# A written-out order of steps whose planner charges for a change between parts of TensorE's array

## The chip, the cores and the metric

The kernel runs on one core of one Trainium2 chip. The metric is the device time in microseconds (us) of one execution; lower is better. PE is the matmul engine (TensorE), DVE is VectorE, ACT is ScalarE, POOL is GpSimd, SP issues DMAs.

## What is computed

The input is x of shape (16, 256, 128), float32. Six parts follow each other, each added to x (LN is a layer norm without weights):

```
x = x + 0.5 * FFN(LN(x))        # ternary weights 128 -> 512 gated (silu * linear), 512 -> 512 gelu, 512 -> 512 gelu, 512 -> 128
x = x + ATT0(LN(x))             # linear attention, no softmax: (theta x)(phi x)^T g(x) / sqrt(128)
x = x + 0.5 * FFN(LN(x))        # the same weights again
x = x + 0.5 * MOE(LN(x))        # 8 low-rank experts, top 2, gates from the first token of each batch
x = x + ATT1(LN(x))             # 16 heads of width 8, rotary, causal softmax over 256 tokens
x = x + 0.5 * MOE(LN(x))
```

## The kernel before

The 16 batches are cut into 8 chunks of 512 tokens (two batches each). The feed-forward layers run as two interleaved streams of chunks; each fp32 product is two matmuls of a rounded high part and a rest (lines 921 and 925). The softmax attention works per batch u in steps of two heads.

Nothing in the kernel decides at run time what comes next. A planner, class `Order`, lays one list of 1,848 steps on the host, and every engine walks this list in the same order and issues its own part of each step, with semaphore waits where data or a buffer is needed. So the list fixes the order on each of the five queues. The planner holds a clock for each engine (`P` for PE, `V` DVE, `A` ACT, `G` POOL, `S` SP). Jobs stand in a list by fixed priorities (a smaller number first; feed-forward about 3, the first pass over the scores 5.5 or 6.5, the maxima 5.2, the second pass 6, the end of a batch 6.6). `run` takes the first job that can go on at the time of `clock["P"]`, the job calls `put` for a step, and `put` moves the clocks by the durations in `TAKES` (for each engine: how long it is held, and how long until the result is there). Whether a bank of PSUM is free, whether a source is done and whether DVE's or ACT's queue is short enough (`pair`: the engine's clock less than `QUEUED` = 1.0 us ahead) are all asked against `clock["P"]`. The kind of array part that a step uses is not asked by any job.

The steps that the change speaks of:

- `pass1` (lines 1075, 1079, 1082), 128 times: 8 bf16 matmuls of 64 or 48 rows for two heads; they use half of the array's rows. DVE then takes the row maxima (line 1315, about 0.95 us) and so empties two banks.
- `pass2` (line 1110), 128 times: 4 bf16 matmuls of 50 rows, the scores transposed, with the maxima as extra rows. ACT takes the exponential (line 1450), POOL masks it (line 1533).
- `weigh` (line 1123), 64 times: 8 fp32 products, 16 matmuls as the trace counts them, of 128 rows and 32 columns: a quarter of the array's columns. They multiply the probabilities with the values for four heads.
- everything else on PE uses the whole array (for instance `upright`, line 1132; `flat`, line 1139; `proj`, 1145; `qk`, 1060; `xta` and the like, 940; `expert`, 1053). `max_out` (line 1099) has 32 columns, but the planner counts it with the whole array.
- `reloc` (DMAs of line 1589): loads K and Q of a batch from DRAM into one of four buffers, ahead of its `pass1` steps; `TAKES` gives it 2.95 us of SP and 5.0 us of DMA.
- `keep` (line 1093): filler. `fill` looks at the stretch in which the planner has PE idle before a step, and lays `int((gap - 0.15) * 0.65 / 0.06)` matmuls of 128x128 on the whole array into it when that is over 1. They compute nothing that is used. `fill` inserts them without passing through `put`, so they move no clock and don't alter `self.pe`, the kind of the last step.

The banks: six banks of PSUM serve as three pairs for the two passes, two more serve all small steps.

Of the kernel before, what the change touches and what calls it, by code (L numbers as in the profile page):

```python
# [30 lines left out]
class Step:  # L31
# [57 lines left out]
COMES = {"stat": [3.5], "cast_v": [5.6, 12.6], "cast_a": [7.1, 8.5, 10.6]}  # L89

BESIDE = ("norm",)
KINDS = {"up": "r", "hid": "r", "down": "r", "pass1": "h", "pass2": "h"}
TABLES = {"silu": "silu", "gelu": "gelu", "pass2": "exp"}
AHEAD = 0.0
KEPT = 4
# [25 lines left out]
class Order:  # L121
# [36 lines left out]
    def put(self, name, **k):  # L158
        n = self.count.get(name, 0)
        self.count[name] = n + 1  # L160
        if name in ("up", "hid", "down"):
            self.into[k["s"]] += 1
            self.lasts = k["s"]
        elif name == "xtf":
            self.into[k["s"]] = 0
        st = Step(name, n, **k)
        self.steps.append(st)
        src = list(st.src) if isinstance(st.src, (list, tuple)) else [st.src]
        if name in ("hid", "down"):
            src = src[st.x:st.x + 2]  # L170
        ready = max([s.at["A"] if s.name in ("cast0", "cast1") else s.done for s in src if s is not None]
                    + [self.left(st.emptied)])
        later = self.left(st.emptied2)
        if n < len(COMES.get(name, ())):
            ready = max(ready, COMES[name][n])
        t = ready
        late = name + "_late" if self.dead and name + "_late" in TAKES else name
        if name == "up" and not self.opened:
            late = "up_first"
        for i, (eng, us, *way) in enumerate(TAKES[late]):  # L180
            if eng == "D":
                t += us
                continue
            if eng == "P":
                kind = KINDS.get(name, "f")
                self.clock["P"] += 0.08 * (kind != "h" and self.pe == "h")
                self.pe = kind
            if eng == "A":
                table = "gelu" if name == "tanh" and self.table == "silu" else TABLES.get(name, self.table)
                self.clock["A"] += 1.29 * (table != self.table)  # L190
                self.table = table
            if i or name == "up":
                t = max(t, later - 0.45 * (name == "up"))
            s0 = max((ready if name in BESIDE else t) + HOPS[eng], self.clock[eng])
            if eng == "P":
                self.fill(s0)
                self.idle_from = s0 + us
            self.note(eng, s0, s0 + us, name)
            self.clock[eng] = s0 + us
            t = st.at[eng] = s0 + way[0]  # L200
        st.done = max([t] + [st.at[e] for e in st.at if name in BESIDE])
        return st
# [1483 lines left out]
```

## Time and profile before

| what | us |
| --- | --- |
| median of 3 runs | 686.41 (686.03 to 687.04) |
| profiled execution, first to last instruction (span) | 684.8 |
| what lies around the span, taken as the median less the span | 1.6 |
| PE busy in the span | 642.0 |
| feed-forward stretch, to the first `pass1` | 0 to 411 |
| attention stretch | 411 to 684.8 |

The profile records no time for its execution other than the span; the 1.6 us of starting and ending are the difference from the median of the runs. Matmuls overlap in the array, so the busy time of PE overstates how long a step holds it. What a step costs is read as the distance from its first start to the next step's first start, in places where PE waited for nothing.

### The profile page before, as it was taken

The page shows a single profiled execution, that of the slowest core. Times are in us where ns is not written, and L with a number is a line of the kernel's source. Part 1 is how long each engine was busy: PE and PEld are TensorE (multiplying, and loading weights), DVE is VectorE, ACT ScalarE, POOL GpSimd, SP SyncE. Part 2 cuts the span into 40 slices and gives each one's busy share as a digit, 9 for nine tenths or more (in the row PEclk, how much of TensorE's full clock was granted, in tenths as well). Part 3 has the DMA queues.
Part 4 walks back from the last instruction along what each step waited for, and adds up shares of the span by engine and source line. Part 5 has one row for each costly group of instructions (what it writes and reads, how often), then busy time and mean ns, then how long its engine had stood idle before and what let it go on. Part 6 is the DMA issues. An engine that isn't in the chain of part 4 may idle for free.

```text
span 684.8 us, 14480 instructions
## 1 busy us (share of the span) xinstructions
PE 642.0 (94%) x5407; PEld 484.4 (71%) x5407; DVE 497.3 (73%) x1300; ACT 493.2 (72%) x846; POOL 300.3 (44%) x461
## 2 busy tenths in 40 slices
PE   4899999999999999999999999889989899999995
PEld 2687878888887878887788877555556565666664
DVE  6767476577566686668786688998897678877455
ACT  5799688778778878877887685248666776567660
POOL 1412121232133363135383637568777653554660
PEclk9999999999999999999999999999999999999999
DMA  9200000000000011000020264414243322112001
GB/s 296 82 1 1 1 0 1 2 0 1 1 0 1 1 46 47 1 1 1 24 69 13 78 199 129 130 48 155 72 151 94 113 93 66 64 49 66 18 2 48
DMA packets 41655, 37.11 MB, mean 54 GB/s; under 512 B 2880, under 2 KB 36960, under 8 KB 41584
## 3 DMA queue, kind: packets, MB, share of 16 engines
q1 hardware_dynamic: 41584, 36.17, 16.9%
q8 instruction: 44, 0.72, 0.4%
q14 instruction: 27, 0.22, 0.1%
HBM read 21.21 MB, written 14.68 MB: 52 GB/s over the span
## 4 chain that ended last, share of the span: by engine, by line
PE 59%; DVE 19%; ACT 10%; issue 6%; DMA 3%; SPq 1%; POOL 1%; DVEq 1%; ACTq 0%; POOLq 0%
PE PSA L921 19%; PE PSA L925 18%; DVE MX L1315 6%; PE PSA L1123 4%; DMA QS<-dq 3%; DVE G L1187 3%; PE PSA L940 3%; PE PSA L1110 2%; ACT PSA L1361 2%; PE PSA L1075 2%; ACT G L1357 2%; PE PSA L1060 1%; ACT PB L1450 1%; DVE RA L1308 1%; PE PSA L1053 1%
## 5 line engine op out<-in xcount | busy, mean ns | idle before, releaser
L1315 DVE TENSOR_REDUCE MX<-PSA 128x6 f32<-128x768 f32 x128 | 118.7, 950 | 25.3 <-PE PSA L1082 24.9
L921 PE MATMUL PSA<-ah,WH 128*128 128x512 f32 x320 | 130.0, 406 | 0.5 <-DVE G L1187 0.5
L925 PE MATMUL PSA<-al,WH 128*128 128x512 f32 x320 | 125.2, 391 | 0.0
L1361 ACT ACTIVATE PSA<-PSA,SC 128x512 f32<-128x512 f32 x128 | 84.7, 662 | 55.0 <-PE PSA L925 54.5
L1450 ACT ACTIVATE PB<-PSA 128x768 f32<-128x768 f32 x128 | 100.7, 815 | 12.8 <-PE PSA L1110 12.5
L921 PE MATMUL PSA<-bh,WH 128*128 128x512 f32 x256 | 104.8, 410 | 2.7 <-DVE G L1187 2.3
L1533 POOL TENSOR_SCALAR_AFFINE_SELECT PB<-PB 128x512 f32<-128x512 f32 x128 | 80.5, 635 | 54.6 <-ACT PB L1450 52.6
L925 PE MATMUL PSA<-bl,WH 128*128 128x512 f32 x256 | 100.3, 392 | 0.0
L1479 POOL TENSOR_SCALAR VE<-MV 128x4 f32<-128x4 f32 x46 | 10.9, 237 | 195.3 <-DVE MV L1162 195.3
L1192 DVE TENSOR_TENSOR al<-PSA,ah 128x512 fp32r<-128x512 f32 x64 | 44.0, 688 | 52.6 <-ACT ah L1368 52.2
L921 PEld LDWEIGHTS PSA<-ah,WH 128*128 128x128 f32 x320 | 60.4, 189 | 13.1 <-issue 0.7
L925 PEld LDWEIGHTS PSA<-al,WH 128*128 128x128 f32 x320 | 60.4, 189 | 12.0 <-issue 0.7
L1192 DVE TENSOR_TENSOR bl<-PSA,bh 128x512 fp32r<-128x512 f32 x64 | 44.0, 688 | 33.6 <-ACT bh L1368 33.3
L1187 DVE SCALAR_TENSOR_TENSOR G<-PSA,SC,G 128x512 f32<-128x512 f32 x64 | 46.8, 748 | 29.6 <-ACT G L1357 22.8
L1489 POOL TENSOR_SCALAR XN<-X,MV,RS 128x128 f32<-128x128 f32 x78 | 62.7, 812 | 3.1
L921 PEld LDWEIGHTS PSA<-bh,WH 128*128 128x128 f32 x256 | 48.1, 188 | 14.0 <-DVE G L1187 4.9
L1123 PE MATMUL PSA<-PB,VA 128*32 128x256 f32 (+1 forms) x1024 | 54.5, 331 | 2.1 <-POOL PB L1533 0.4
L925 PEld LDWEIGHTS PSA<-bl,WH 128*128 128x128 f32 x256 | 48.2, 188 | 8.9 <-issue 0.2
L921 PE MATMUL PSA<-XH,WH 128*128 128x512 f32 x128 | 53.2, 416 | 1.4 <-DVE XL L1182 1.4
L1463 ACT ACTIVATE OT<-PSA 128x256 f32<-128x256 f32 x64 | 24.7, 386 | 38.1 <-PE PSA L1123 38.0
L925 PE MATMUL PSA<-XL,WH 128*128 128x512 f32 x128 | 51.1, 399 | 0.0
L1481 POOL TENSOR_TENSOR RS<-VE,MHALF 128x4 f32<-128x4 f32 x46 | 48.4, 1053 | 3.8
(148 smaller groups left out, 1354.3 us busy)
## 6 DMA issues: line engine op xcount, KB each, us to landing
KS<-dk SPq DMA_DIRECT2D x32, 192.0 KB
QS<-dq SPq DMA_DIRECT2D x32, 192.0 KB
dk<-CB SPq DMA_DIRECT2D x16, 192.0 KB, 2.6
dq<-CB SPq DMA_DIRECT2D x16, 192.0 KB, 2.3
X<-in_x SPq DMA_DIRECT2D x8, 256.0 KB, 6.8
dk<-CB SPq DMA_DIRECT2D x16, 128.0 KB, 2.1
dq<-CB SPq DMA_DIRECT2D x16, 128.0 KB, 1.9
VA<-in_ones SPq DMA_DIRECT2D x4, 512.0 KB
```

Of the source, the lines that this page charges most:

```text
L921: e.matmul(o, WH[:, col:col + 128], hi, start=first, stop=False)
L925: return e.matmul(o, WH[:, col:col + 128], low, start=False, stop=last)
L1123: t = e.matmul(PSA[32 * v:32 * v + 32, b, 128 * k:256], V[:, k, 4 * g + v, :], P[:, 1, :] if k else P[:, 0::2, :], start=(k == 0), stop=(k ...
L1187: e.scalar_tensor_tensor(out=G[:, i, :], in0=bank(b), scalar=SC[:, 4 + st.j:5 + st.j], in1=G[:, i, :], op0=ALU.mult, op1=ALU.mult).then_in ...
L1192: e.tensor_tensor(cut(PL_[st.s, dst], st.j), h, cut(PH_[st.s, dst], st.j), ALU.subtract).then_inc(v_lo, 1)
L1315: e.tensor_reduce(MX[:, u % 2, 1:4, :].rearrange("p t (l g) -> p l t g", l=2)[:, :, :, g], PSA[:, b:b + 2, 0:384].rearrange("p l (t k) -> ...
L1361: e.activation(bank(b), bank(b), ACT.Gelu, scale=SC[:, k:k + 1]).then_inc(a_gelu, 1)
L1450: e.activation(PB[:, n % 4, :, :, :].rearrange("p t l q -> p l t q"), PSA[:, b:b + 2, 0:384].rearrange("p l (t q) -> p l t q", t=3), ACT.E ...
L1463: e.activation(OT[u % 2][:, g, :], PSA[:, b, 0:256], ACT.Copy).then_inc(a_ot, 1)
L1481: e.tensor_tensor(RS[:, i, :], VE[:, i, :], MHALF[:, :], ALU.pow).then_inc(g_rs, 1)
L1489: t = e.tensor_scalar(XN[:, i, j, :], X[:, 4 * c + j, :], MV[:, i, j, 0:1], RS[:, i, j:j + 1], ALU.subtract, ALU.mult)
L1533: e.affine_select(out=P, in_=P, compare_op=ALU.is_ge, fill=0.0, base=0, pattern=[[0, 4], [1, 128]], channel_multiplier=-1).then_inc(g_sel, 1)
```

## The change

Three things change in the planner, none in what a step does:

1. Before, `put` moved PE's clock on by 0.08 us when a step that isn't `pass1` or `pass2` followed one of these. Now it moves it by 0.094 us whenever the kind of the part differs from that of the step before, in either direction, with three kinds: half (`pass1`, `pass2`), quarter (`weigh`), whole (all others).
2. `pass1` is planned 0.01 us shorter on PE (0.34), `pass2` 0.01 us shorter (0.17).
3. `weigh` is planned 0.10 us shorter on PE (0.69), and its result 0.08 us earlier (0.78).

The entries `up`, `hid` and `down` of the old table had the kind "r", which only had to differ from "h".

```diff
--- before.py
+++ after.py
@@ -75,10 +75,10 @@
     "cast1": [("A", 0.52, 0.62), ("S", 0.95, 0.95), ("D", 2.5)],
     "rest1": [("G", 1.12, 1.16), ("S", 0.95, 0.95), ("D", 2.3)], "reloc": [("S", 2.95, 2.95), ("D", 5.0)],
     "value": [("P", 0.83, 1.05), ("A", 0.48, 0.59)], "vexp": [("A", 0.31, 0.41)], "ones": [("S", 1.5, 1.5), ("D", 6.0)],
-    "pass1": [("P", 0.35, 0.51), ("V", 0.868, 0.95)], "peak": [("V", 0.14, 0.22), ("A", 0.13, 0.24), ("G", 0.2, 0.26)],
+    "pass1": [("P", 0.34, 0.51), ("V", 0.868, 0.95)], "peak": [("V", 0.14, 0.22), ("A", 0.13, 0.24), ("G", 0.2, 0.26)],
     "max_out": [("P", 0.22, 0.29), ("V", 0.2, 0.27), ("S", 1.18, 1.18), ("D", 3.8)],
-    "pass2": [("P", 0.18, 0.34), ("A", 0.69, 0.81), ("G", 0.59, 0.63)],
-    "weigh": [("P", 0.79, 0.86), ("A", 0.27, 0.38)], "upright": [("P", 0.45, 0.6), ("V", 0.5, 0.58)],
+    "pass2": [("P", 0.17, 0.34), ("A", 0.69, 0.81), ("G", 0.59, 0.63)],
+    "weigh": [("P", 0.69, 0.78), ("A", 0.27, 0.38)], "upright": [("P", 0.45, 0.6), ("V", 0.5, 0.58)],
     "flat": [("P", 0.27, 0.44), ("A", 0.27, 0.38)], "proj": [("P", 0.64, 0.71), ("V", 0.33, 0.41)], "store": [("S", 0.9, 0.9)],
     "half_stat": [("V", 0.7, 0.8)], "half_power": [("G", 1.1, 1.1)], "half_norm": [("V", 0.45, 0.5)], "half_xt": [("P", 0.2, 0.6), ("A", 0.27, 0.38)],
     "half_logit": [("P", 0.2, 0.4), ("V", 0.5, 0.6)], "half_tanh": [("A", 0.09, 0.2)], "half_pick": [("V", 1.3, 1.4)],
@@ -89,7 +89,7 @@
 COMES = {"stat": [3.5], "cast_v": [5.6, 12.6], "cast_a": [7.1, 8.5, 10.6]}
 
 BESIDE = ("norm",)
-KINDS = {"up": "r", "hid": "r", "down": "r", "pass1": "h", "pass2": "h"}
+TILES = {"pass1": "h", "pass2": "h", "weigh": "q"}
 TABLES = {"silu": "silu", "gelu": "gelu", "pass2": "exp"}
 AHEAD = 0.0
 KEPT = 4
@@ -182,8 +182,8 @@
                 t += us
                 continue
             if eng == "P":
-                kind = KINDS.get(name, "f")
-                self.clock["P"] += 0.08 * (kind != "h" and self.pe == "h")
+                kind = TILES.get(name, "f")
+                self.clock["P"] += 0.094 * (kind != self.pe)
                 self.pe = kind
             if eng == "A":
                 table = "gelu" if name == "tanh" and self.table == "silu" else TABLES.get(name, self.table)
```

## Rows read from the trace of the kernel before

**Rows 1.** The page: span, busy share of each engine, granted clock in 40 slices

```profile
span 684.8 us, 14480 instructions
...
PE 642.0 (94%) x5407; PEld 484.4 (71%) x5407; DVE 497.3 (73%) x1300; ACT 493.2 (72%) x846; POOL 300.3 (44%) x461
...
PEclk9999999999999999999999999999999999999999
```

**Rows 2.** Busy us of each engine in four stretches (start:end, length, then engines)

```profile
0.00:410.00 410.00, 393.06 (x1985) 320.76 (x1986) 283.23 (x739) 326.34 (x521) 135.60 (x195) 1.00 0.12 36
410.00:440.00 30.00, 27.77 (x248) 20.32 (x246) 27.30 (x79) 12.59 (x23) 21.43 (x32) 1.00 0.44 144
440.00:640.00 200.00, 186.05 (x2744) 118.37 (x2742) 164.25 (x377) 134.03 (x258) 125.42 (x205) 1.00 0.27 85
640.00:684.80 44.80, 35.10 (x438) 24.99 (x436) 22.48 (x108) 20.24 (x45) 17.84 (x31) 0.98 0.09 26
```

**Rows 3.** Filler after 410 us, from instructions of PE by line (busy, mean | idle)

```profile
L1093 PE MATMUL PSA<-IDB 128*128 128x128 bf16 x316 | 27.6, 220 | 0.2
```

**Rows 4.** Line 1075: duration min/median/max, first and last start

```profile
L1075 PE MATMUL PSA<-MK,IM x512: 213/242/281, 411.7 to 636.2; 64*128 64x128 bf16 x86, 64*128 64x256 bf16 x85
```

**Rows 5.** PE in order of time: start, duration, line (five places)

```profile
445.29 0.34 PE L1075 MATMUL PSA<-MK,IM 64*128 64x256 bf16 x4
...
445.73 0.34 PE L1093 MATMUL PSA<-IDB 128*128 128x128 bf16 x3
446.00 0.34 PE L1075 MATMUL PSA<-MK,IM 64*128 64x256 bf16 x4
...
465.00 0.86 PE L1123 MATMUL PSA<-PB,VA 128*32 128x256 f32 x16
465.79 0.34 PE L1110 MATMUL PSA<-QS,KS 50*128 50x256 bf16 x4
...
466.39 0.66 PE L1132 MATMUL PSA<-IDN,OT 128*128 128x128 f32 x4
466.98 0.34 PE L1110 MATMUL PSA<-QS,KS 50*128 50x256 bf16 x4
...
478.99 0.34 PE L1110 MATMUL PSA<-QS,KS 50*128 50x256 bf16 x4
479.17 0.33 PE L1075 MATMUL PSA<-MK,IM 64*128 64x256 bf16 x4
...
479.51 0.33 PE L1075 MATMUL PSA<-MK,IM 64*128 64x256 bf16 x4
...
479.93 0.66 PE L1132 MATMUL PSA<-IDN,OT 128*128 128x128 f32 x4
...
557.24 0.60 PE L1132 MATMUL PSA<-IDN,OT 128*128 128x128 f32 x4
557.68 0.44 PE L1093 MATMUL PSA<-IDB 128*128 128x128 bf16 x5
```

**Rows 6.** Waits between 440 and 640 us: total, times, longest

```profile
POOL PB L1533 <- ACT PB L1450: 44.9, 51, 3.0
...
DVE MX L1315 <- PE PSA L1082: 24.9, 37, 2.6
...
PEld PSA L1110 <- issue: 10.1, 47, 0.8
```

**Rows 7.** The chain that ended last, 440 to 640 us: shares by line

```profile
by line: DVE MX L1315 17.9%; PE PSA L1123 12.5%; DMA QS<-dq 9.8%; PE PSA L1110 6.7%; issue 6.1%; PE PSA L1075 5.4%; ACT PB L1450 3.3%; DVE RA L1308 3.1%; SPq L1589 2.9%; PE PSA L1082 2.6%; PE PSA L1060 2.2%; PE PSA L1132 1.7%; PE PSA L1145 
```

**Rows 8.** The same chain in order of time, 616 to 627 us

```profile
617.24 0.74 SPq L1589
...
618.75 6.57 DMA QS<-dq
...
625.36 0.34 PE PSA L1075 x4
```

## The prediction

> **What bounds the kernel now.** I read the page first, then the four stretches, then the waits and the chain, and last PE in order of time. The page gives a span of 684.8 us with PE busy 94% and its clock fully granted in all slices [rows 1]. The busy share doesn't say that PE is the limit everywhere. In the stretches [rows 2], PE is busy 393 of the first 410 us, where the feed-forward runs. From 440 to 640 us, in the attention, it is busy 186 of 200 us, but this counts matmuls that overlap, and part of it is filler: 316 filler matmuls stand after 410 us [rows 3]. DVE is at 164 of 200 there (82%), ACT at 134, POOL at 125. So no engine is full; the engines wait for each other's results. POOL waits 44.9 us for ACT's exponentials, DVE 24.9 us for `pass1`, 37 times, and PE's weight loads before `pass2` stand 10.1 us in "issue" [rows 6]. The chain agrees [rows 7]: DVE's maxima have 17.9% of this stretch, `weigh` 12.5%, the loading of K and Q 9.8% (with 2.9% to issue it), `pass2` 6.7%, `pass1` 5.4 + 2.6% and its third line, "issue" 6.1%. Counting PE's lines shown and "issue", about 40% lies on PE, and I call it half with the lines that aren't shown.
>
> **What the change does to the list.** The price is added to `clock["P"]`; no job asks for the kind. So the planner doesn't group steps of one kind, and nothing in the edit lowers the number of changes. It only makes PE slower in the plan, and so other jobs are found ready, and other banks free, at other points. The first `pass1` comes at 411.7 us [rows 4]. Before it every step uses the whole array, so no change is charged; the one exception is the very first step, whose kind differs from the empty one, and there PE's clock is overtaken by the wait for the input. The first 411 us of 684.8 therefore stay as they are, step for step.
>
> **Is the new price the true one?** Distances from start to start, PE waiting for nothing [rows 5]: `pass1` followed by a half step holds PE 0.34 us (479.17 to 479.51), followed by a whole one 0.42 (479.51 to 479.93) or 0.44 (445.29 to 445.73). A change costs 0.08 to 0.10. `pass2` to `pass1` is 0.18 (478.99 to 479.17). `weigh` to `pass2` is 0.79 (465.00 to 465.79); planned now 0.69 + 0.094 = 0.784. In the other direction `upright` to filler is 0.44 (557.24 to 557.68) and `upright` to `pass2` 0.59 (466.39 to 466.98): 0.15. So the change is dear both ways, and the old planner charged it one way only, except for `weigh`, where it was inside the 0.79. The new table is nearly right, and still 0.05 low after a whole step.
>
> The Trainium skill says the same in kind: changing the tiling mode drains TensorE ("TensorEngine Tiling (Array Packing)", Tiling Modes, Key Properties), and "TensorE: Matmul & The Clock Gate" ("Step-by-step: what each phase is for") puts the drain through the array at 128 cycles, an estimate of 0.053 us at 2.4 GHz. By that figure 345 changes would cost 18 us; by the 0.09 of the rows they cost 31 us. I go by the rows.
>
> **The sum of the prices.** Following PE's steps along the trace, I count 345 changes: 103 whole to half, 118 half to whole, 55 quarter to half, 40 half to quarter, 22 and 7 between whole and quarter. Fillers stand in that stream but aren't seen by the planner; without them 306 remain, of which 142 leave a half step. For this same list the old planner charged 142 x 0.08 = 11.4 us, and the new one charges 306 x 0.094 = 28.8 us. The shorter table takes back 256 x 0.01 + 64 x 0.10 = 9.0 us. Net, PE's clock runs 28.8 - 11.4 - 9.0 = 8.4 us more over the 273 us of the attention, 3%. The chip pays these 8.4 us already, in both kernels; they are no cost of the edit.
>
> **Where a gain can come from.** Filler is laid where the planner has PE idle. A planned clock that is short by a price takes PE to be idle for longer than it is, and the filler then delays the next step. At 445.73 three fillers go between two `pass1` steps and hold PE for 0.27 us with no wait after them, and they bring a change on each side: the `pass1` before cost 0.44 instead of 0.34 [rows 5]. About half of the 8.4 us falls where PE waits in the plan (the half above), so some 4.2 us of planned idleness goes. One us of planned idleness lays 0.65/0.06 = 10.8 fillers; one filler holds PE (0.27 - 0.09)/3 = 0.06 us, so 0.65 us. That is 4.2 x 0.65 = 2.7 us less filler. With it some batches fall away: the 316 fillers stand in 60 batches, 5.3 in each, which is about 0.49 us of planned idleness beyond the 0.15; so 4.2/0.64 = 6 batches, two changes of 0.09 each, 1.1 us. Together 3.8 us of PE's work. It counts only where PE sets the pace, again half: 1.9 us. The bounds: nothing, if the batches that fall away were covered by real waits; and, if all 8.4 us were idle time and all of PE's work counted, 8.4 x 0.65 + 13 x 0.18 = 7.8 us.
>
> I set nothing against it for the new order in itself: a step put earlier or later moves waits of both signs. It is the larger unknown, though. The stretch has 37 waits of DVE for `pass1`, 24.9 us in all [rows 6], 0.67 us each; four of them more or fewer on the chain are 2.7 us either way.
>
> No instruction is added or removed but fillers: the same DMAs, the same 128 + 128 + 64 attention steps. The DMAs of `reloc` move with their step on SP's queue, and with them the later stores of rotated K and Q that stand behind them.
>
> **The rivals.**
>
> *The order moves little, or its moves cancel.* Then the time is that of before, 686.4. For it: 60% of the span is untouched, priorities are fixed, and each batch's steps follow from the data. Against: readiness is a yes or no at a time, and a clock 3% slower turns many of these answers.
>
> *A load of K and Q lands late.* One loading has 8.1 us from its first issue to the first `pass1` (617.24 to 625.36), of which 6.57 is the DMA on the chain [rows 8]; the planner takes 7.95. Three such stretches stand on the chain, the 9.8% of 200 us, 19.6 us. With the old prices PE ran slower than planned, so a load had more real time than planned under the same list. The new clock takes this spare away: it puts `pass1` right where it expects the landing. One more load that stands bare, less what PE does meanwhile (take half of 8.1), is 4 us: 690.5. It decides when `reloc` comes over 0.2 us later against the work ahead of it than now, the difference of 8.1 and 7.95. This is the rival on the slower side.
>
> *The price is still wrong where it matters.* `proj`, `qk` and `value` may have been planned with part of a change inside their times (`proj` 0.64, `value` 0.83), and now pay 0.094 on top; `max_out` uses 32 columns and is taken for a whole step. The plan is then too slow there, PE arrives early and waits. 16 `max_out` and 16 `proj` at 0.09 are at most 2.9 us of plan, and half of them on the chain 1.4 us slower: 687.8.
>
> *Less filler lets the clock fall.* The granted share is 1.00 to 640 us and 0.98 after it [rows 2]. If a short stretch fell to 1.2 GHz, a batch's end of some 4 us of PE work would take 4 us more: 690.4. PE is busy 35 of the last 44.8 us, so I hold this unlikely.
>
> **How the numbers follow.** The forecast is the span of 684.8 less 1.9, and 1.6 around it: 684.5 against the median of 686.41, 0.3% faster. Faster by the filler and kinder waits: 0.42. No difference: 0.25. A late load or a worse order: 0.22. The price wrong at small steps: 0.07. The clock: 0.04. All under 0.2% of the time (1.4 us) can't be told from no change. The last three are slower ones, 0.33 together; of the forecast nearly all is faster, of the second rival a third stays within the bound. So faster 0.43, same 0.26, slower 0.31. The forecast's own range is 681.5 to 686. The range over the cases reaches from 680.5 (two thirds of the bound of 7.8 us, or the filler with four waits fewer) to 691 (a bare load and a little).
>
> **What would show it.** Right: PE's stream identical up to 411 us; fewer fillers than 316 after 410 us, with more of the rest standing before real waits; about 345 changes still, within 15; DVE's waits for `pass1` at or below 24.9 us. Wrong: a stretch of the loading DMA on the chain beyond 19.6 us, more "issue", or the same number of fillers. If the number of changes falls by 30 or more, the gain comes from luck in the order and not from the way that I describe. If DVE between 440 and 640 us goes well above 82%, the order was better for DVE and the filler had little to do with it.

## The result and the profile after

The changed kernel is slower: 690.11 us median (688.8 to 693.39, 6 runs) against 686.75 us (686.03 to 688.26, 6 runs); the ratio is 1.0048 with a 95% interval of 1.0029 to 1.0067. The forecast was 684.5 us and its range was wide enough (680.5 to 691), but the side was the wrong one. The profiled execution took 688.8 us, of which the span is 687.1: 2.3 us over the span of before.

The page of the changed kernel (the rows that answer to [rows 1]):

```profile
span 687.1 us, 14619 instructions
...
PE 643.4 (94%) x5474; PEld 487.4 (71%) x5474; DVE 498.4 (73%) x1300; ACT 491.4 (72%) x846; POOL 301.2 (44%) x461
...
PEclk9999999999999999999999999999999999999999
```

DVE, ACT and POOL issue as many instructions as before. PE issues 67 more, and these are filler: 383 after 410 us where [rows 3] had 316 (PE by line, from 410 us to the end, changed kernel; columns: count, busy us, mean ns, idle us before):

```profile
L1093 PE MATMUL PSA<-IDB 128*128 128x128 bf16 x383 | 33.0, 220 | 0.0
```

The four stretches, as in [rows 2]: start and end, length, then the busy time of PE, weight loads, DVE, ACT, POOL, the granted clock, and the DMA engines' busy share and GB/s.

```profile
0.00:410.00 410.00, 393.21 (x1986) 320.14 (x1987) 282.99 (x739) 326.42 (x521) 136.29 (x195) 1.00 0.12 36
410.00:440.00 30.00, 27.94 (x252) 20.52 (x250) 27.21 (x81) 12.60 (x23) 21.57 (x32) 1.00 0.44 144
440.00:640.00 200.00, 186.42 (x2800) 120.02 (x2798) 161.90 (x362) 132.12 (x257) 124.16 (x200) 1.00 0.27 85
640.00:687.10 47.10, 35.87 (x443) 26.74 (x442) 26.30 (x122) 20.22 (x46) 19.14 (x35) 0.98 0.08 24
```

The first stretch is the same within 0.3 us on every engine but for the weight loads' 0.6 and POOL's rough 0.7. The loss is made from 440 to 640 us. There PE is as busy as before, but what it feeds did less: ACT 132.1 us of work instead of 134.0, DVE 161.9 instead of 164.3, POOL 124.2 instead of 125.4. That work is then left for the end, which takes 47.1 us instead of 44.8. Since the first three stretches have a fixed length, the last one must show the whole 2.3 us of span; the work left over at 640 us says where they come from.

One finer stretch of the fillers alone (line 1093; columns: busy time of PE and of weight loads, the granted clock, DMA), changed kernel first, then before, shows where 55 of the 67 went in: between 440 and 540 us. From 540 to 640 us the two have 58 and 59.

```profile
440.00:540.00 100.00, 12.77 (x159) 9.34 (x156) 1.00 0.35 105
```

```profile
440.00:540.00 100.00, 9.41 (x104) 5.92 (x101) 1.00 0.33 102
```

The waits of the changed kernel between 440 and 640 us answer to [rows 6], and the chain's shares there to [rows 7]:

```profile
POOL PB L1533 <- ACT PB L1450: 48.1, 44, 3.0
DVE MX L1315 <- PE PSA L1082: 26.7, 36, 2.0
...
PEld PSA L1110 <- issue: 9.0, 46, 0.2
```

```profile
by line: PE PSA L1123 16.8%; DVE MX L1315 12.8%; PE PSA L1075 8.2%; PE PSA L1110 6.5%; DMA QS<-dq 6.5%; issue 4.6%; ACT PB L1450 4.1%; PE PSA L1082 3.7%; PE PSA L1060 3.3%; ACT OT L1463 2.2%; POOL PB L1533 2.1%; PE PSA L1093 2.1%; PE PSA L9
```

The chain has moved from DVE and the DMA to PE: the loading of K and Q has 6.5% of 200 us where it had 9.8%. The filler itself stands on the chain now with 2.1%.

PE's stream, counted step by step as for the forecast, has 316 changes between array parts instead of 345 (83 whole to half, 105 half to whole, 59 and 37 between quarter and half, 27 and 5 between whole and quarter). At 0.094 us each, 29 changes fewer give back 2.7 us. The kernel became slower all the same.

### The profile page after: what moved, and what is told of

Its sections match the earlier page's. It is cut to its first block, busy times and chain, and to the rows that moved or that the text cites. A ratio compares the mean times of both kernels' runs of the same rounds, so it can differ in the third digit from the quotient of the medians.

```text
span 687.1 us, 14619 instructions
## 1 busy us (share of the span) xinstructions
PE 643.4 (94%) x5474; PEld 487.4 (71%) x5474; DVE 498.4 (73%) x1300; ACT 491.4 (72%) x846; POOL 301.2 (44%) x461
## 4 chain that ended last, share of the span: by engine, by line
PE 63%; DVE 15%; ACT 10%; issue 5%; DMA 3%; POOL 2%; SPq 1%; DVEq 1%; ACTq 0%
PE PSA L921 19%; PE PSA L925 18%; PE PSA L1123 6%; DVE MX L1315 5%; DVE G L1187 3%; PE PSA L940 3%; PE PSA L1075 2%; PE PSA L1110 2%; DMA QS<-dq 2%; PE PSA L1060 2%; ACT PSA L1361 2%; PE PSA L1053 2%; ACT PB L1450 1%; ACT G L1357 1%; PE PSA L1093 1%
## 5 line engine op out<-in xcount | busy, mean ns | idle before, releaser
L1315 DVE TENSOR_REDUCE MX<-PSA 128x6 f32<-128x768 f32 x128 | 118.5, 950 | 26.9 <-PE PSA L1082 26.7
L1450 ACT ACTIVATE PB<-PSA 128x768 f32<-128x768 f32 x128 | 99.3, 818 | 7.7 <-PE PSA L1110 7.5
L1368 ACT ACTIVATE ah<-G 128x512 fp32r<-128x512 f32 x64 | 40.4, 631 | 13.1 <-DVE G L1187 13.0
```

Source lines behind the costliest of these rows:

```text
L1315: e.tensor_reduce(MX[:, u % 2, 1:4, :].rearrange("p t (l g) -> p l t g", l=2)[:, :, :, g], PSA[:, b:b + 2, 0:384].rearrange("p l (t k) -> ...
L1368: e.activation(cut(PH_[st.s, dst], st.j), G[:, i, :] if g == 0 else bank(b), ACT.Copy).then_inc(a_hi, 1)
L1450: e.activation(PB[:, n % 4, :, :, :].rearrange("p t l q -> p l t q"), PSA[:, b:b + 2, 0:384].rearrange("p l (t q) -> p l t q", t=3), ACT.E ...
```

## The experiments

All ratios are against the kernel before on the same chip, with 95% intervals. For the later runs I also used a **reckoning**: the finished list is run through the planner's clocks once more, always at the prices and durations of the changed kernel (0.094 us), whatever the planner that made it believed. It is no measurement; it says which of two lists ought to end first. It leaves the fillers out altogether, for they move no clock.

### The two halves of the change, and the price moved a little

```diff
-                self.clock["P"] += 0.094 * (kind != self.pe)
+                self.clock["P"] += 0.093 * (kind != self.pe)
```

> The price is 0.093 us instead of 0.094, everything else as in the changed kernel. Over 306 changes the plan differs by 0.3 us in price, but the list that comes out is another one: its fillers after the first pass over the scores rise from 337 to about 430 and the planner's own end from 675.9 to 685.6. Theory 1 (every list is a draw, and the time is that of the list): 5 to 10 us slower than the changed kernel, some 695 to 700. Theory 2 (a price close to the truth takes slack away and that is what costs): the same as the changed kernel within 1 us, 690. Theory 3 (filler on PE is the loss): some 85 fillers at 0.06 us and their changes, at most 5 us slower, 692 to 695.

Measured: 696.83 us, ratio 1.0141 (1.0111 to 1.0171). One thousandth of a microsecond in the price made 6 to 7 us, twice the change under study. Theory 2 falls. Filler isn't excluded by this run alone: the list has 87 fillers more than the changed one, an estimated 5.2 us at the forecast's 0.06 us each if every one of them delayed real work. The stretches of this kernel show where (changed kernel first, then the 0.093 one; columns as above):

```profile
410.00:520.00 110.00, 102.54 (x1348) 67.07 (x1348) 98.53 (x226) 64.01 (x119) 79.31 (x115) 1.00 0.36 113
520.00:580.00 60.00, 55.41 (x834) 36.45 (x832) 47.10 (x116) 39.08 (x79) 34.38 (x59) 1.00 0.28 89
580.00:640.00 60.00, 56.40 (x881) 37.02 (x873) 43.48 (x100) 41.62 (x83) 32.04 (x58) 1.00 0.18 60
```

```profile
410.00:520.00 110.00, 102.48 (x1349) 67.22 (x1349) 98.55 (x226) 63.86 (x119) 79.14 (x115) 1.00 0.36 112
520.00:580.00 60.00, 55.63 (x843) 37.18 (x843) 44.25 (x107) 39.09 (x79) 34.27 (x59) 1.00 0.27 85
580.00:640.00 60.00, 56.16 (x856) 36.64 (x845) 43.51 (x105) 37.71 (x75) 28.65 (x53) 1.00 0.19 64
```

Up to 520 us the two are the same to 0.2 us. In the two lists, fillers aside, the first difference is that the `tanh` of chunk 0 stands behind `value` and `max_out` instead of before them. From there DVE does 2.9 us less work than in the changed kernel by 580 us, and ACT 3.9 us less from 580 to 640. (The fillers in my expectation were counted too low: the traces have 383 and 470.)

Without any price, the short table kept:

```diff
-                self.clock["P"] += 0.094 * (kind != self.pe)
+                self.clock["P"] += 0.0 * (kind != self.pe)
```

> No price for a change at all, the shorter table of the changed kernel kept. The planner's PE is then 29 us too fast over the attention. Theory 1: the planner's fault in the price matters little against the draw; the list is a middling one, 685 to 690. Theory 2: with the most slack of all this is faster than the changed kernel and at or below the kernel before, 684 to 687. My failed forecast would say the opposite of both: the most filler in the wrong places, over 692.

Measured: 687.6 us, ratio 1.0007 (0.999 to 1.0025): no difference from before, and nowhere near the 692 that my forecast's reasoning called for. Its 377 fillers, 61 more than before, cost nothing that shows.

The new charge alone, with the old table of durations (against the kernel before, whose table it keeps):

```diff
-KINDS = {"up": "r", "hid": "r", "down": "r", "pass1": "h", "pass2": "h"}
+TILES = {"pass1": "h", "pass2": "h", "weigh": "q"}
...
-                kind = KINDS.get(name, "f")
-                self.clock["P"] += 0.08 * (kind != "h" and self.pe == "h")
+                kind = TILES.get(name, "f")
+                self.clock["P"] += 0.094 * (kind != self.pe)
```

> The new charge with the table of before. weigh then pays for its change twice (0.79 and 0.094). Theory 1: the list has more filler still and a planned end of 686.5, so slower than the changed kernel by 3 to 8 us, 693 to 698. Theory 2 (closeness to the truth costs): the plan is 6 us too slow for weigh and so less true; no worse than the changed kernel, 686 to 690.

Measured: 694.7 us, ratio 1.0119 (1.0084 to 1.0154).

The short table alone, with the old charge (against the changed kernel):

```diff
-TILES = {"pass1": "h", "pass2": "h", "weigh": "q"}
+KINDS = {"up": "r", "hid": "r", "down": "r", "pass1": "h", "pass2": "h"}
...
-                kind = TILES.get(name, "f")
-                self.clock["P"] += 0.094 * (kind != self.pe)
+                kind = KINDS.get(name, "f")
+                self.clock["P"] += 0.08 * (kind != "h" and self.pe == "h")
```

> The shorter table with the charge of before: half of the change alone. Theory 1: also a new list, with 425 fillers against 313 in the list of before (the planner's count after the first pass1), and so slower than before by 2 to 6 us, 689 to 692, though the new charge isn't in it. Theory 2: the charge is what matters, so this is like before, 685.5 to 687.5.

Measured: 690.57 us, ratio 1.0051 (1.0032 to 1.0069). Each half of the change by itself costs as much as the whole or more. They don't add up: 1.2% and 0.5% together make 0.5%.

### Without filler

```diff
     order = Order()
+    first1 = next(i for i, st in enumerate(order.steps) if st.name == "pass1")
+    order.steps = [st for i, st in enumerate(order.steps) if st.name != "keep" or i < first1 - 1]
```

> The list of the changed kernel with every filler from the first pass over the scores on left out; nothing else moves, for fillers move no clock of the planner. Theory 3 (the added filler is the loss): 3 us and more faster than the changed kernel, and within 1 us of the list of before without filler. Theory 1 (the order of the real steps is the loss): filler mostly fills real waits, so at most 1.5 us faster than the changed kernel, and the list of before without filler is still 2 to 4 us ahead. If the clock of PE falls without filler, both are slower than with it.

> The list of the kernel before with the same fillers left out. Theory 3: 1 to 3 us faster than before, 684 to 686. Theory 1: within 1 us of before, 685.5 to 687.5, and 2 to 4 us faster than the changed list without filler.

Measured: 692.76 us (1.0064, 1.0036 to 1.0093) for the changed list and 693.85 us (1.0076, 1.0052 to 1.01) for that of before. The list of before lost 0.8%. The loss of the changed list can't be told from the 1.0048 that it has with filler. Both theories missed: without filler the list of before is not the 2 to 4 us ahead that theory 1 called for, and neither list got faster, as theory 3 would have it. What came is the other thing that I had written down: the clock fell, and neither list is faster than with filler. The stretch from 440 to 640 us and the rest, of the changed list and then that of before, both without filler:

```profile
440.00:640.00 200.00, 178.03 (x2542) 111.37 (x2540) 158.98 (x358) 129.35 (x252) 121.77 (x196) 0.94 0.27 85
640.00:690.90 50.90, 34.81 (x378) 24.19 (x372) 27.78 (x123) 23.04 (x51) 20.98 (x38) 0.84 0.08 23
```

```profile
440.00:640.00 200.00, 178.00 (x2496) 109.81 (x2492) 159.08 (x362) 130.03 (x248) 120.61 (x194) 0.93 0.27 85
640.00:693.70 53.70, 39.51 (x424) 26.03 (x424) 27.74 (x127) 25.45 (x55) 22.90 (x42) 0.83 0.07 21
```

The granted clock is 0.94 and 0.93 in the middle and 0.84 and 0.83 at the end, against 1.00 and 0.98 with filler. Part of the time PE ran at 1.2 GHz, the lower of its two levels. In the changed list without filler the clock fell after PE had been busy 1.28 of 2 us and less (PE alone: busy time, then the granted clock and DMA):

```profile
432.00:434.00 2.00, 1.28 (x20) 1.00 0.38 135
436.00:438.00 2.00, 2.00 (x21) 0.50 0.48 139
```

The Trainium skill has this rule ("TensorE: Matmul & The Clock Gate", What's actually happening: the throttled state is the default and activity lifts it), and these rows agree: 1.00 before, 0.50 after the stretch with less work. So for the list of before the filler pays. Whether 67 more or fewer cost anything these two runs can't say, since the fall of the clock covers it, and it fell further for the list of before (a mean of 0.962 to 0.974 in its runs, 0.966 to 0.977 for the changed list). The table further down says more of theory 3.

### The order at the end

> The changed kernel with one step moved: the statistics of batch 13's last part stand before the logits of batch 12's last part on DVE, as they do in the list of before, so that the expert choice of batch 12 doesn't queue behind them. In the profile of the changed kernel that choice starts at 668.35 us, 3.7 us later than before, while the last projection comes only 0.3 us later; all that follows on DVE is serial. If the tail's order on DVE holds the loss: 1 to 2 us faster than the changed kernel, 688 to 689. If the loss sits earlier, in the 200 us before, and the tail only passes it on: within 0.5 us of the changed kernel.

```diff
+    order.steps.insert(at("half_logit", 12), order.steps.pop(at("half_stat", 13)))
```

Measured: 689.46 us, ratio 1.0027 (1.0013 to 1.004), where the changed kernel had 1.0048 on another chip. The intervals overlap. The difference, 0.2% or some 1.4 us, would be of the size that the tail theory called for, but what it named didn't happen: the choice began at 668.5 us, no earlier than the 668.3 of the changed kernel. So I ran the changed kernel again beside a stronger form:

> The changed kernel once more, unedited, on the chip on which the next two run, so that they can be set against it directly. 0.3 to 0.6% slower than before, a span near 687 us.

> The changed kernel with two steps of its last part moved: the gates and the expert choice of batch 12 stand directly behind that batch's logits on ACT and DVE, ahead of the statistics of batch 13 and of the last transposes of batch 15, as near as in the list of before. In the profile of the changed kernel this choice begins at 668.35 us against 664.66 before, and the four choices follow one another on DVE. If the order of the tail on DVE makes the last 2 us of the loss: the choice begins near 666.5 and the kernel is 1 to 2 us faster than the changed one of the same chip. If the tail only hands on what came late from the 200 us before it: within 0.5 us of the changed one.

```diff
+    for name in ("half_tanh", "half_pick"):
+        order.steps.insert(at("half_stat", 13), order.steps.pop(at(name, 12)))
```

Measured on one chip: 690.11 us (1.006, 1.0034 to 1.0085) for the changed kernel, 692.01 us (1.007, 1.0048 to 1.0092) with the choice ahead. The gates of the choice (line 1286, DVE: duration, then first and last start), unedited and then edited:

```profile
L1286 DVE TENSOR_SCALAR GS<-TT x4: 153/154/154, 669.8 to 683.4; 128x1 f32<-128x1 f32 x4
```

```profile
L1286 DVE TENSOR_SCALAR GS<-TT x4: 153/154/154, 668.1 to 685.0; 128x1 f32<-128x1 f32 x4
```

The first choice begins 1.7 us earlier and the last one 1.6 us later. In between, PE's clock fell, which no theory had in it (edited kernel, PE alone: busy time, then the granted clock and DMA):

```profile
672.00:674.00 2.00, 2.00 (x11) 0.50 0.00 0
```

In the edited kernel PE was busy 0.38 us of the two from 668 and 0.79 of the two from 670; then the granted clock was 0.80, 0.50 and 0.85 in the stretches from 670 to 676 us, where the unedited kernel had 1.00. An estimate from these shares is up to 1.7 us of PE work lost, as much as the last choice is late. So this edit doesn't test the order alone, and the tail theory is neither shown nor excluded; what is shown is that work is missing before the tail begins, by 640 us. The reckoning gives the two edits little, too: 672.4 and 673.8, against 672.9 unedited.

### Is the time a property of the list?

Five lists, by constants alone. Against the kernel before (0.083 in the same place for the second):

```diff
-                self.clock["P"] += 0.08 * (kind != "h" and self.pe == "h")
+                self.clock["P"] += 0.079 * (kind != "h" and self.pe == "h")
```

> The kernel before with 0.079 us in place of its 0.08. Run through the planner's clocks at the changed kernel's prices (durations of the table, no measurement), the lists so far end at 668.7 (before), 670.2 (price 0), 672.9 (changed), 675.4 (shorter table alone), 679.8 (new charge, old table) and 682.6 (price 0.093), and the measured medians lie 0, 0.5, 3.3, 3.5, 8.2 and 9.7 us above before: about 0.7 us for each. This list ends at 666.5. Theory 1 (the time is that of the list, and a list can jump at 0.001 us): 1 to 2 us faster than before. Theory 2 (what counts is how far the price is from the truth): no difference.

> The kernel before with 0.083 us in place of 0.08. The same reckoning ends at 676.7. Theory 1: 4 to 7 us slower than before, as much as or more than the change under study, though the form of the charge is the old one. Theory 2: 0.4 us of price over the whole list, no difference.

Against the changed kernel:

```diff
-QUEUED = 1.0
+QUEUED = 0.8
```

> The changed kernel with the limit on how far DVE's or ACT's planned queue may run ahead of PE set from 1.0 to 0.8 us. The reckoning ends at 669.1 against 672.9 of the changed kernel. If the new prices are at fault in themselves: as slow as the changed kernel, 3 us over before. If the other constants were fitted to the old clock and the true price only undid the fit: within 1 us of before.

The changed kernel with `0.0895 *` for `0.094 *`:

> The changed kernel with 0.0895 us in place of 0.094. The reckoning ends at 676.8, near the mean of 25 prices from 0.088 to 0.1 (677.6, with a spread of 2.1; 0.094 itself has the lowest, 672.9). Theory 1 with the list's own time: 5 to 7 us slower than before, so that the change under study was a good draw of its kind. Theory 2: between before and the changed kernel, 2 to 3.5 us slower than before.

Against the kernel before:

```diff
-QUEUED = 1.0
-LEAD = 12
+QUEUED = 0.7
+LEAD = 16
...
-                self.clock["P"] += 0.08 * (kind != "h" and self.pe == "h")
+                self.clock["P"] += 0.078 * (kind != "h" and self.pe == "h")
```

> A list picked by the reckoning alone, out of 224 made with other prices, queue limits (QUEUED) and leads (LEAD): the charge of before with 0.078 us, QUEUED 0.7, LEAD 16. It ends at 664.8 against 668.7 of before and 666.5 of the 0.079 list, which measured 0.36% faster. If the time of a list is its own and the reckoning carries over at 0.7 us for each: 2 to 4 us faster than before, 0.3 to 0.6%. If picking the lowest of many only picks the reckoning's errors: no better than the 0.079 list, 0 to 0.3% faster.

| list | reckoning | measured us (ratio, interval) | fillers after 410 us |
| --- | --- | --- | --- |
| best_list | 664.8 | 682.65 (0.9935, 0.9914 to 0.9956) | 318 |
| old charge, 0.079 | 666.5 | 684.65 (0.9964, 0.9951 to 0.9976) | 309 |
| before (0.08) | 668.7 | 1 | 316 |
| new charge, QUEUED 0.8 | 669.1 | 685.6 (0.9986, 0.9973 to 0.9998) | 345 |
| no price | 670.2 | 687.6 (1.0007) | 377 |
| changed (0.094) | 672.9 | 690.11 (1.0048) | 383 |
| short table alone | 675.4 | 690.57 (1.0051) | 428 |
| old charge, 0.083 | 676.7 | 693.6 (1.01, 1.0073 to 1.0127) | 414 |
| new charge, 0.0895 | 676.8 | 693.14 (1.0093, 1.0075 to 1.0112) | 417 |
| new charge, old table | 679.8 | 694.7 (1.0119) | 416 |
| new charge, 0.093 | 682.6 | 696.83 (1.0141) | 470 |

The reckoning gives the order of the measured ratios, with two near ties turned round (668.7 and 669.1, 676.7 and 676.8). The five lists of this part were run after the others were known, and each came where the reckoning put it; best_list and the 0.079 list were even a little better. The number of fillers ranks the lists less well: the short table alone has 428 of them and is 0.5% slower, the old charge with 0.083 has 414 and is 1% slower; the list without a price and the changed kernel have 377 and 383 and are 0.4% apart, as the reckoning, which holds no filler, has them. So the order of the real steps explains the times, and theory 3 isn't needed for them. The price of before moved by 0.001 us gives a kernel 0.36% faster, moved by 0.003 us one that is 1% slower, in the same form of charge. And the new prices with one constant moved are not slower than before (new_queue08).

Between 440 and 640 us the span goes with the work that gets through. The list picked last, and that with 0.093, from 440 to 640 us:

```profile
440.00:640.00 200.00, 188.91 (x2837) 122.22 (x2834) 166.24 (x384) 137.71 (x263) 126.46 (x207) 1.00 0.27 84
```

```profile
440.00:640.00 200.00, 186.34 (x2785) 120.53 (x2783) 159.08 (x359) 128.08 (x249) 120.50 (x195) 1.00 0.27 85
```

ACT's work in the 200 us is 137.7, 134.0, 132.1 and 128.1 us for the spans 681.2, 684.8, 687.1 and 694.2, and over all eleven lists of the table it falls nearly in the order in which the spans grow. PE's busy time is nearly the same in all of them (189, 186, 186, 186 us) and says little.

## Why the prediction was wrong

- **The first 411 us stay as they are.** Right: 393.2 against 393.1 us of PE, same counts on ACT, DVE and POOL.
- **The new price is nearly the true one, and the chip pays it either way.** The rows of before showed 0.08 to 0.10 us from a half step to a whole one and 0.15 the other way, and no run contradicts them. But that the plan is truer has no worth of its own: 0.093 is as true as 0.094 and costs 6 to 7 us more.
- **The planner doesn't group steps by kind.** Right in mechanism. The changes still fell, by 29, where I had allowed 15. That is 2.7 us less of PE's time, and the kernel lost all the same.
- **Less planned idle time, so less filler.** This is the step that failed first. I held the list fixed and let only the planned gaps shrink: 4.2 us less idle, some 45 fillers fewer. In truth the lists part near the planner's 440 us, and the new one has 67 fillers more; at the forecast's 10.8 fillers for each us that is an estimated 6.2 us more planned idle time instead of 4.2 less. The two lists with about as many fillers as before (309, 318) are the two that are clearly faster, and none with 377 or more is faster, so their number goes with the idle time that a list leaves. That filler is a cost was the other half of this step. No run shows it: 61 fillers more in price_0 cost nothing that shows, and taking all of it out made both lists no faster and one clearly slower, with a lower clock.
- **"I set nothing against it for the new order in itself."** This was the term that decided, and I took it as zero with 2.7 us to either side. Over the ten lists of the table other than before, the times lie from 4 us below it to 10 us above. The reckoning of 25 prices from 0.088 to 0.1 has a mean of 677.6 with a spread of 2.1, and 25 from 0.074 to 0.086 in the old form 671.7 with 3.3. Before (668.7) is a good draw among its neighbours, so a change of anything was likelier to lose. But the loss isn't only a draw: the means of the two forms are 5.9 apart, more than either spread, and the changed kernel, the best of its 25 in the reckoning, is still behind before. The constants around the price were presumably set with the old clock, which nothing here records. new_queue08 shows that with one of them, `QUEUED`, moved from 1.0 to 0.8 the loss is gone in one list; in the reckoning the 25 prices of the new form then have a mean of 671.4 and the 25 of the old form 672.0. The old form has its good mean at 1.0 only among its neighbours: 13 of its prices have 677.3 at 0.9 and 677.5 at 1.1. So the gap belongs to the pair of form and constant, and not to the new prices in themselves. In the sum, the term that stood at 0 measured the whole loss of 3.3 us, and the 1.9 us of the filler show in no run.
- **A late load of K and Q.** Didn't come: its share of the chain fell from 9.8% to 6.5% of the 200 us. **The clock.** Didn't fall: 0.98 at the end in both. **The price still wrong at small steps.** Not tried by itself. None of the rivals had the right mechanism; the two that ended at 690.5 and 690.4 had the right time by chance.
- **What would show it.** The signs were well chosen in one point: fillers not fewer, DVE's waits for `pass1` over 24.9 us (26.7) both said wrong. The others said nothing: neither the loading nor "issue" grew on the chain.

What stays open: by what way a slower PE clock in the plan together with `QUEUED` = 1.0 makes worse lists. The means with `QUEUED` = 0.8 are reckoned, and only one list with it and the new prices was measured; which of the planner's choices it changes for the better isn't settled.

## What to carry to other kernels

A greedy planner with yes-or-no readiness is in part a lottery in its inputs: a constant changed by 1% gives another list, and here the lists differ by 2% of the whole time. Judge a change of such a constant by the spread of its neighbours, not by one list against a single good one, and retune the constants that were set beside the old value: here the neighbours' mean moved by more than their spread, and one such constant took that back in the reckoning and in the one list measured. And if the planner's model is good enough to rank lists, use it for that: make a few hundred with slightly different constants, run each through one fixed set of prices, and time the best; this gave 0.65% here, when a truer price alone gave a loss.

## What the runs showed of the hardware

- Leaving out the 316 fillers of the list of before, which compute nothing, made it 0.8% slower: the granted clock was 0.93 from 440 to 640 us and 0.83 after it, against 1.00 and 0.98.
- In the changed kernel with the choice moved forward, PE was busy 0.38 and 0.79 us of two stretches of 2 us, and the granted clock, 1.00 before, was 0.50 from 672 to 674 us, with PE busy all of that time.
- The same program, the changed one, had profiled spans of 687.1 and 688.3 us on two chips, so a single profile can't tell differences of 1 us.
